# A recurrence of 256 small steps: the scan's multiplying operand and the tanh of the cell move from SBUF to PSUM

## The reference, cut to what matters

```python
B, T, _ = x.shape                       # 8 images, 256 tokens, 64 channels
xi = xt @ U_i + b_i                     # the same for xf, xg, xo
def step(carry, xs):
    h, c = carry
    xi_t, xf_t, xg_t, xo_t = xs
    i_t = sigmoid(xi_t + h @ V_i)
    g_t = tanh(xg_t + h @ V_c)
    o_t = sigmoid(xo_t + h @ V_o)
    c_new = h * c + i_t * g_t
    h_new = o_t * tanh(c_new)
    return ((h_new, c_new), h_new)
(_, _), hs = lax.scan(step, (h0, c0), (xi, xf, xg, xo))
```

## Time and profile before

| | |
|---|---|
| median of 3 runs | 982.26 us (981.43 to 983.58) |
| the profiled execution's own time | 980.65 us |
| its span, first to last instruction | 978.9 us |
| mean granted TensorE clock | 0.755 |
| busy share of the span: PE, DVE, ACT, POOL | 79%, 56%, 57%, 38% |
| first start of L724, last start of L1072 | 146.4 us, 568.6 us |

### The profile page before, as it was taken

One profiled execution on the slowest core, in us unless ns is written; L12 is line 12 of the kernel. 1 busy time (PEld: TensorE's weight loads), 2 busy tenths in 40 slices (PEclk: granted clock), 3 DMA queues, 4 the chain that ended last, 5 costly groups with the idle time before them and its releaser, 6 DMA issues.

```text
span 978.9 us, 18102 instructions
## 1 busy us (share of the span) xinstructions
PE 768.5 (79%) x6224; PEld 572.3 (58%) x6224; DVE 552.2 (56%) x1558; ACT 554.3 (57%) x1579; POOL 369.5 (38%) x296
## 2 busy tenths in 40 slices
PE   6899986666666666666666468999869999899996
PEld 3578875555555555555555445778736666466663
DVE  3788744555355355333333337887466676567665
ACT  3677743333355355333333336767558888688884
POOL 0877710000000000000000008777158888588884
PEclk9999985555555555555555559999879999899999
DMA  9600000000001100000000000000000010100001
GB/s 224 164 2 1 3 1 1 1 1 1 0 1 76 76 1 1 1 1 1 1 1 0 1 0 1 2 1 2 1 1 2 1 77 2 78 2 1 2 1 23
DMA packets 5861, 18.54 MB, mean 19 GB/s; under 512 B 1093, under 2 KB 2822, under 8 KB 5254
## 3 DMA queue, kind: packets, MB, share of 16 engines
q1 hardware_dynamic: 5478, 17.21, 6.0%
q10 hardware_dynamic: 288, 0.13, 0.1%
HBM read 9.47 MB, written 0.52 MB: 10 GB/s over the span
## 4 chain that ended last, share of the span: by engine, by line
PE 36%; POOL 21%; DVE 15%; ACT 12%; issue 12%; DVEq 1%; POOLq 1%; DMA 0%; SPq 0%; ACTq 0%
POOL zw L829 21%; PE bank L470 10%; PE bank L472 6%; DVE bank L1068 6%; PE bank L339 5%; ACT scan_io L724 5%; PE bank L356 5%; ACT tcell L728 5%; PE bank L304 5%; DVE hr L1072 4%; DVE hid L904 2%; PE bank L277 1%; PE bank L326 1%; PE bank L272 1%; PE bank L369 1%
## 5 line engine op out<-in xcount | busy, mean ns | idle before, releaser
L789 POOL TENSOR_TENSOR st<-tent,tentx 128x768 f32<-128x768 f32 x96 | 150.8, 1604 | 510.5 <-DVE tentx L897 500.0
L829 POOL TENSOR_TENSOR zw<-hid,zw 128x512 f16<-128x512 f32 x176 | 203.9, 1159 | 49.3 <-ACT zw L756 36.0
L470 PE MATMUL bank<-hr,lv 64*64 64x8 f32 x512 | 97.2, 262 | 151.1 <-DVE hr L1072 151.1
L470 PEld LDWEIGHTS bank<-hr,lv 64*64 64x64 f32 x512 | 73.0, 202 | 197.7 <-DVE hr L1072 197.6
L1171 DVE SCALAR_TENSOR_TENSOR hid<-bank,wsc,st 128x512 f32<-128x512 f32 x176 | 132.0, 750 | 75.7 <-ACT st L760 70.3
L724 ACT ACTIVATE scan_io<-bank 64x16 f32<-64x16 f32 x256 | 47.6, 186 | 216.6 <-PE bank L472 216.4
L510 PE MATMUL bank<-st,wh 128*128 128x512 f16 x352 | 136.8, 389 | 11.9 <-POOL st L822 5.4
L760 ACT ACTIVATE st<-bank,wsc 128x512 f32<-128x512 f32 x176 | 121.0, 687 | 40.1 <-PE bank L511 22.4
L1068 DVE TENSOR_TENSOR_SCAN bank<-scan_io 64x24 f32<-64x24 f32 x256 | 53.0, 207 | 157.8 <-ACT scan_io L724 157.7
L511 PE MATMUL bank<-st,wl 128*128 128x512 f16 x352 | 136.5, 388 | 0.0
L525 PEld LDWEIGHTS bank<-w2p,zw 128*128 128x128 f16 x1408 | 97.0, 98 | 45.4 <-POOL zw L829 4.1
(11 more groups left out here) (145 smaller groups left out, 1130.0 us busy)
## 6 DMA issues: line engine op xcount, KB each, us to landing
w13s<-w SPq DMA_DIRECT2D x8, 704.0 KB, 15.8
w2f<-w SPq DMA_DIRECT2D x4, 384.0 KB, 25.6
w13s<-wh SPq DMA_DIRECT2D x2, 704.0 KB, 3.4
w13s<-wl SPq DMA_DIRECT2D x2, 704.0 KB, 4.5
wh<-w13s SPq DMA_DIRECT2D x2, 704.0 KB, 3.8
wl<-w13s SPq DMA_DIRECT2D x2, 704.0 KB, 5.1
w2f<-w2p SPq DMA_DIRECT2D x2, 384.0 KB, 4.8
w2p<-w2f SPq DMA_DIRECT2D x2, 384.0 KB, 5.7
```

What stands on the lines that cost most here:

```text
L470: nc.tensor.matmul(both[:, 0, t, :], lv[:, C:2 * C], prev, start=False, stop=True, skip_group_check=True)
L789: nc.gpsimd.tensor_tensor(st[p][:, t, k:k + KG, :].rearrange("p k (y x) -> p k y x", x=16), ty, tx, ALU.mult)\
L829: nc.gpsimd.tensor_tensor(hl[:, u % MR, :], hid[:, u % MR, :], hh[:, u % MR, :], ALU.subtract)\
```

## The change

`scan_io` is gone. The scan's multiplying operand is now `gates`, 24 columns of PSUM bank 0, of which ACT writes elements 1 and 2 of each image; its added operand is `scan_add`, an SBUF tile of 24 columns that holds (1, 1, kept). The state of an image is then 1, tanh i + 1, and tanh c * (1 + tanh i) + kept: the same cell. `tcell` is now 8 columns of PSUM bank 1. The zeros among the multipliers are written once by DVE, behind the last product of `norm(1)`, and ACT's first step waits for them. As banks 0 and 1 are in use during the recurrence, the transposes and the product for the experts' scales go to bank 2. Every engine has the same instructions in the same order as before, apart from the one DVE memset. In the changed kernel the lines are 4 lower up to that memset and 2 lower behind it: L724 becomes L720, L726 becomes L722, L728 becomes L724, L1068 becomes L1066, L1072 becomes L1070 and L1076 becomes L1074.

```diff
-        scan_io = sb("scan_io", [C, 2 * B * 3 + 8])
+        scan_add = sb("scan_add", [C, B, 3])
         cell = bank[7][0:C, 0:B * 3].rearrange("p (b k) -> p b k", k=3)
-        scan_add = scan_io[:, 0:24]
-        scan_mul = scan_io[:, 26:50]
-        scan_one = scan_io[:, 0:52].rearrange("p (a n) -> p a n", a=2)[:, :, 0:24] \
-            .rearrange("p a (b k) -> p a b k", k=3)[:, :, :, 1]
-        scan_ig = scan_io[:, 0:56].rearrange("p (a n) -> p a n", a=2)[:, :, 0:24] \
-            .rearrange("p a (b k) -> p a b k", k=3)[:, :, :, 0]
-        scan_hc = scan_add.rearrange("p (b k) -> p b k", k=3)[:, :, 2]
-        tcell = sb("tcell", [C, B])
+        gates = bank[0][0:C, 0:B * 3]
+        gate_in = gates.rearrange("p (b k) -> p k b", k=3)
+        kept = scan_add[:, :, 2]
+        tcell = bank[1][0:C, 0:B]
...
             def largest_weights():
                 pe.wait_ge(s("w_max"), 2)
                 for k in range(2):
-                    nc.tensor.transpose(bank[0][0:1, k * 128:k * 128 + 128], wmax[:, k:k + 1], ident[:, :])\
+                    nc.tensor.transpose(bank[2][0:1, k * 128:k * 128 + 128], wmax[:, k:k + 1], ident[:, :])\
                         .then_inc(s("w_tr"), 1)
...
-                nc.tensor.matmul(bank[1][:, 0:2], ones[:, :], wpow[:, 2, :], start=True, stop=True)\
+                nc.tensor.matmul(bank[2][:, 256:258], ones[:, :], wpow[:, 2, :], start=True, stop=True)\
                     .then_inc(s("w_bc"), 1)
...
-            act.wait_ge(s("l_init"), 3)
+            act.wait_ge(s("l_zero"), 1)
             for n in range(STEPS):
...
-                nc.scalar.activation(scan_ig, both, ACT.Tanh).then_inc(s("l_act"), 1)
+                nc.scalar.activation(gate_in[:, 1:3, :], both, ACT.Tanh).then_inc(s("l_act"), 1)
...
             nc.vector.memset(ones[:, :], 1.0).then_inc(s("l_init"), 1)
-            nc.vector.memset(scan_io[:, :], 0.0).then_inc(s("l_init"), 1)
+            nc.vector.memset(scan_add[:, :, :], 1.0).then_inc(s("l_init"), 1)
             dve.wait_ge(s("l_init"), 2)
-            nc.vector.memset(scan_one, 1.0).then_inc(s("l_init"), 1)
+            nc.vector.memset(kept, 0.0).then_inc(s("l_init"), 1)
...
             norm(1)
+            dve.wait_ge(s("n1_xn"), 1)
+            nc.vector.memset(gates, 0.0).then_inc(s("l_zero"), 1)
...
                 nc.vector.tensor_tensor_scan(cell[:, :, :].rearrange("p b k -> p (b k)"),
-                                             scan_mul, scan_add, 0.0, ALU.mult, ALU.add).then_inc(s("l_c"), 1)
+                                             gates, scan_add[:, :, :].rearrange("p b k -> p (b k)"), 0.0, ALU.mult, ALU.add).then_inc(s("l_c"), 1)
...
-                    nc.vector.scalar_tensor_tensor(out=scan_hc, in0=hr[:, n % (2 * W), :], scalar=0.5,
+                    nc.vector.scalar_tensor_tensor(out=kept, in0=hr[:, n % (2 * W), :], scalar=0.5,
                                                    in1=cell[:, :, 2], op0=ALU.mult, op1=ALU.mult)\
```

More of the change, by code:

```diff
@@ L198, in build @@
                   "w_part", "w_max", "w_tr", "w_pow", "w_bc", "w_scale", "w_fac", "w_high", "w_split", "w_stored", "l_scaled",
-                  "l_gi", "l_o", "l_act", "l_oact", "l_c", "l_tc", "l_h", "l_hc", "l_up", "l_res", "l_init",
+                  "l_gi", "l_o", "l_act", "l_oact", "l_c", "l_tc", "l_h", "l_hc", "l_up", "l_res", "l_init", "l_zero",
                   "m_w0", "m_w1", "m_high", "m_scaled", "m_parts", "m_log", "m_max", "m_exp", "m_sm", "m_ge",
@@ L1011, in scales @@
                 elif k == 4:
-                    power("w", wpow, bank[0], WTOP)
+                    power("w", wpow, bank[2], WTOP)
                 elif k == 9:
                     dve.wait_ge(s("w_bc"), 1)
-                    nc.vector.tensor_copy(wsc[:, 2:4], bank[1][:, 0:2]).then_inc(s("w_scale"), 1)
+                    nc.vector.tensor_copy(wsc[:, 2:4], bank[2][:, 256:258]).then_inc(s("w_scale"), 1)
                 elif k == 10:
-                    nc.vector.reciprocal(wsc[:, 0:2], bank[1][:, 0:2]).then_inc(s("w_scale"), 1)
+                    nc.vector.reciprocal(wsc[:, 0:2], bank[2][:, 256:258]).then_inc(s("w_scale"), 1)
                 elif k == 11:
```

## The result

The changed kernel takes 966.12 us, the median of 4 runs (965.92 to 966.52), against 982.31 us (981.43 to 983.58, 4 runs, one more than in the table of the kernel before): a ratio of 0.9839, 95% interval 0.9823 to 0.9854. The profiled execution's span is 964.1 us. The forecast was 965.0 us with a range of 956.5 to 976.

What follows compares the result with a forecast made beforehand. The prediction took the latency of small operations in the recurrence's step as the bound: 256 x (34 + 34 + 0 + 0) = 17.4 us, less 0.1, gives 17.3; 982.26 - 17.3 = 965.0 us, range 956.5 to 976.

Steps and rivals of the forecast that it cites:

- a ring of latencies: Recurrence step: gates' tanh, scan, cell's tanh, h, PE, one engine at a time; 1.64 us, 256 times.
- (a): ACT's gates' tanh (L724) writes PSUM in place of SBUF: 34 ns saved a step, ends 0 and 50.
- (b): ACT's tanh of the cell (L728) writes PSUM in place of SBUF: 34 ns saved a step, ends 0 and 50.
- (c): DVE's scan (L1068) reads its multipliers from PSUM: 0, ends -2 and +12 ns.
- (d): DVE's h (L1072) reads tanh of the cell from PSUM: 0, ends -2 and +12 ns.
- (e): PE's stretch and the gaps between engines keep the same instructions and waits; L1076 still reads and writes what it did.
- (f): Work hidden in engines' idle time: PE's 0.23 us before L470 falls to 0.16; two held-up steps lose 0.1 us together.
- (g): Added DVE memset of 24 columns behind norm(1): its like takes 72 ns, over 2 us cover it.
- No change: Rival: ACT's end takes as long from either memory, time within 2 us of 982.3; chance 0.09.
- Slower by DVE's reads: Rival: DVE pays for PSUM reads at L1068 and L1072, 8.2 us slower, 990.5, or up to 1007.9; chance 0.07.
- Half a gain: Rival: writes save 15 to 20 ns, or DVE's reads cost 12 each; 971.0 to 979.7 us; chance 0.16.
- The clock: Rival: PE's granted clock rises above 0.50 in the recurrence, some 77 us saved, 888 us; chance 0.02.

Runs made afterwards that it cites:

- The strides' runs: Changed kernel with tanh of the cell written to every third word, one run each: in SBUF 974.3 us, in PSUM 964.61 us.

## Why the prediction was right

*What bounds the kernel.* Right: the step is a ring of latencies, and only what shortened an operation on it counted. 64 ns a step became 16.5 us.

*(a) The gates' write.* Forecast 34 ns, measured 33. The size was right, half by luck: the read side was taken as the measure for the write side, and the stride as free in both memories. The strides' runs put 24 ns on the memory and, by the working above, some 9 on a stride that costs ACT time in SBUF alone.

*(b) The cell's write.* Forecast 34, measured 24. This is the term that was mis-sized: the write side is nearer to PSUM by less than the read side was (34 ns in the pair of copies of the earlier trace rows). By the Trainium skill's figures (Perfetto Trace Analysis, "Optimizing Scalar/DVE Operations") it would have been 42 ns for each write and 21.5 us in all; the trace shows 24 for a write without a stride. The page's direction is right, its size is too large for this write; of the two read pairs in the earlier trace rows the like one, 34 ns, lies below it and the unlike one, 50 ns, above.

*(c) and (d) DVE's reads.* Forecast 0 each. The scan's is 0 (207 ns in both). h's is 5 ns shorter, beyond the end of -2 that was given; by luck it made up for half of what (b) lacked. Sum of the durations: 33 + 24 + 5 = 62 ns, where 68 were forecast; the step shows 64. The other 2 ns are spread over the gaps and PE's stretch, about 1 ns or less at each.

*(e) The pieces that stay.* Right in the sense that they did not change. Wrong if read as fixed: two of the gaps can be shortened by 0.07 us each, together twice what the change brought, and it takes only another order of two waits. In the earlier trace rows there are 0.09 us between 301.63 + 0.20 and 301.92, beside 0.03 and 0.04 us in the earlier trace rows, where DVE has one wait, and the prediction did not ask why. The chain of the kernel before has the same three pieces there:

```profile
301.82 0.03 issue
301.85 0.02 DVEq L1067
301.87 0.04 issue
```

*(f) The cover.* Right: PE's idle time before the next product in a step with the bias product is 0.17 us, forecast 0.16 (timeline of the changed kernel):

```profile
507.77 0.68 PE L428 MATMUL bank<-ones,lb 1*64 1x128 f32 x2
508.62 0.38 PE L466 MATMUL bank<-hr,lv 64*64 64x8 f32 x2 [0.17 <-DVE hr L1070]
```

The step that PE's scale product holds up takes 1.86 us as before, so it lost its gain. The prediction counted a second such step, at DVE's scales (L944), and that reading was wrong: the chain passes through them, but the scan behind them started on time (steps of 1.65 us before and 1.58 after). The five or three steps of about 2 us were not in the prediction; they moved 0.6 us.

*(g) The memset.* It takes 78 ns and ends more than 2 us before the first gates' tanh needs it.

*The rivals.* No change: ruled out by the result and by the rows of L720 and L724. Slower by DVE's reads: ruled out by the run with the gates alone in SBUF (scan 208 ns, not less) and by that with the cell's tanh alone in SBUF (h 159 ns, more than 154). The table in the Trainium skill's VectorE: DVE Perf Modes, "The TRN2 errata", whose 62 cycles more for PSUM spoke for it, does not fit these pairs (207 against 208 ns for the scan, 154 against 159 for h); in both the other operand stays in SBUF. Half a gain: the cell's write alone went part of that way. The clock: 0.50 throughout.

## What to carry to other kernels

Where small operations wait for one another on several engines, as in this ring, the time is the sum of their durations and of the gaps between them. Here an intermediate that ACT writes and DVE reads once was better off in PSUM, where a bank was free, and the strided one the more so; this was measured for 8 and 16 words a partition only. In such a ring the gaps in the chain deserve the same accounting as the durations. Where an instruction has two waits, look for the engine's queue on the chain at the line of the second one, and write the wait that comes last in time first; here that alone took the kernel to 947 us, and with the change to 931.

## What the runs showed of the hardware

- The order of two waits ahead of one DVE instruction was worth 0.07 us each time: 0.09 to 0.10 us from ACT's end to DVE's start with the late wait second, 0.03 with it first. In the first case the chain has a piece of DVE's queue at the second wait's line, in the other none. That the queue handles the second wait as an instruction of its own is how I read these pieces; no run tested it further.
- ACT wrote 8 neighbouring words to PSUM 24 ns faster than to SBUF (147 against 171 ns). A jump of three words cost it 5 ns in SBUF and nothing in PSUM.
- DVE's operation on 8 columns was 5 ns shorter with tanh of the cell in PSUM (154 against 159 ns), and its scan of 24 columns took the same with its multipliers in either (207 and 208 ns).
- A few steps of the recurrence took 0.35 us longer, each behind a piece of DVE's queue: five before, and the same three in the changed kernel and every variant of it that only moved a tile. The late instruction is always one that stands 64 places into a block of 128 of DVE's records. With both pairs of waits swapped, two of the three stay, late by 0.23 and 0.25 us, and in the kernel before four of the five, by 0.17 or 0.18. In the variant that drops one wait and swaps the other pair, whose list is one record a step shorter, no step stands out in this way. Why these places stays open.
